# Attention and a routed feed-forward layer on one core: square roots, exponentials and turns moved in the last two stages

## The reference, cut to what matters

```python
# x: (4, 512, 256) fp32; attention: 16 query heads, 4 key/value heads, D = 128
q, k, v = x @ Wq, x @ Wk, x @ Wv              # k and v repeated for 4 query heads each
y     = softmax(rope(q) @ rope(k).T * D**-0.5, causal) @ v
o_gla = scan over t of  S = S * exp(g_t) + ks_t v_t ;  o_t = qs_t S
        # qs, ks = softmax of q, k over D;  g = log_sigmoid(k) / 16
x = layernorm(x + (0.5 * y + 0.5 * o_gla) @ Wo)
# feed-forward: 8 experts, each 256 -> 176 -> 256, a token takes its top 2
w = softmax(x @ gate_w.T);  top_w, top_i = top_k(w, 2)
f = sum over the 2 experts of  top_w * ((silu(x @ Wg) * (x @ Wu)) @ Wd)
x = layernorm(x + f)                          # (v - mean) / sqrt(var + 1e-5)
```

## Time and profile before

| | us |
|---|---|
| median of 3 runs | 973.99 (973.38 to 974.23) |
| the profiled execution | 972.46 |
| its span in the trace | 970.6 |
| PE busy | 925.6 (95%) |
| ACT busy | 661.7 (68%) |
| DVE busy | 653.2 (67%) |
| POOL busy | 634.5 (65%) |
| mean granted PE clock | 0.985 of full |

### The profile page before, as it was taken

How to read it: one execution, slowest core, us unless ns; L and a number is a source line. 1 busy time by engine, 2 the same in 40 slices (tenths; PEclk the granted TensorE clock), 3 DMA queues, 4 the chain that set the end, 5 groups by cost and what they waited for, 6 DMA issues and landing times.

```text
span 970.6 us, 18411 instructions
## 1 busy us (share of the span) xinstructions
PE 925.6 (95%) x5347; PEld 717.4 (74%) x5347; DVE 653.2 (67%) x1598; ACT 661.7 (68%) x2138; POOL 634.5 (65%) x609
## 2 busy tenths in 40 slices
PE   7899999999999999999999999999999988998991
PEld 4677778787878787878878777777778766776770
DVE  4776767676767676767676969676978774452284
ACT  6677777777777777777777767786768674454452
POOL 6868685767565657676767768775658883536452
PEclk9899999999999999999999999999999999999996
DMA  7101100000000000900000000010102111233363
GB/s 252 34 17 34 39 1 1 7 12 6 1 0 0 0 0 6 252 18 1 1 2 1 1 6 8 1 63 1 63 2 74 50 59 55 82 89 118 111 197 114
DMA packets 34066, 43.20 MB, mean 45 GB/s; under 512 B 3772, under 2 KB 27966, under 8 KB 33856
## 3 DMA queue, kind: packets, MB, share of 16 engines
q1 hardware_dynamic: 30240, 33.76, 12.0%
q0 software_dynamic: 3744, 8.43, 2.5%
HBM read 25.58 MB, written 18.43 MB: 45 GB/s over the span
## 4 chain that ended last, share of the span: by engine, by line
PE 86%; ACT 4%; DVE 4%; issue 3%; DMA 2%; POOL 1%; another core or an unknown queue 0%; POOLq 0%; SPq 0%; DVEq 0%; ACTq 0%
PE OA L597 13%; PE PR L480 12%; PE S L550 11%; PE MS L570 10%; PE S L579 7%; PE S L696 5%; PE OA L559 5%; PE OA L713 4%; PE OA L590 4%; PE PR L526 3%; PE PR L520 3%; PE S L541 1%; PE MS L509 1%; DMA acc<-in_x_rows 1%; ACT eqk L828 1%
## 5 line engine op out<-in xcount | busy, mean ns | idle before, releaser
L1500 POOL TENSOR_TENSOR qd<-eqk,eg 128x512 f32<-128x512 f32 x63 | 74.9, 1189 | 161.8 <-issue 155.4
L597 PE MATMUL OA<-wT,V 128*128 128x512 f32 x320 | 149.2, 597 | 0.0
L790 ACT ACTIVATE S<-S,nm 128x128 f32<-128x128 f32 (+3 forms) x256 | 126.9, 496 | 28.7 <-DVE nm L1003 25.4
L828 ACT ACTIVATE eqk<-qkv,nmx 128x128 f32<-128x128 f32 x320 | 124.4, 396 | 3.4 <-DVE nmx L1078 2.9
L1003 DVE TENSOR_REDUCE nm<-S 128x2 f32<-128x256 f32 (+3 forms) x128 | 102.0, 817 | 30.7 <-PE S L550 24.7
L1488 POOL TENSOR_TENSOR eqk<-eqk,rse 128x640 f32<-128x640 f32 x63 | 79.6, 1264 | 52.8 <-DVE rse L1121 31.5
L597 PEld LDWEIGHTS OA<-wT,V 128*128 128x128 f32 x320 | 59.7, 191 | 69.4 <-issue 68.9
L1037 DVE TENSOR_TENSOR pr<-S,rl 128x256 f32<-128x256 f32 (+3 forms) x128 | 105.5, 824 | 5.0
L1477 POOL TENSOR_TENSOR rp<-qkv,cos 128x640 f32<-128x640 f32 x64 | 99.6, 1556 | 6.6 <-ACT qkv L818 4.9
L1480 POOL TENSOR_TENSOR rp<-rp,rt 128x640 f32<-128x640 f32 x64 | 99.6, 1556 | 5.0
L1477 POOL TENSOR_TENSOR rt<-qkv,sin 128x640 f32<-128x640 f32 x64 | 99.3, 1552 | 0.0
(11 more groups left out here) (174 smaller groups left out, 2499.4 us busy)
## 6 DMA issues: line engine op xcount, KB each, us to landing
qkv<-slot_x SPq DMA_DIRECT2D x46, 129.0 KB
pr<-plane SPq DMA_DIRECT2D x16, 256.0 KB, 2.8
gu_w<-in_wgu SPq DMA_DIRECT2D x8, 352.0 KB, 3.4
slot_x<-zero SPq DMA_DIRECT2D x2, 1290.0 KB, 9.4
stage<-in_wqkv SPq DMA_DIRECT2D x6, 384.0 KB, 3.5
xraw<-in_x_cols SPq DMA_DIRECT2D x16, 128.0 KB, 2.4
acc<-in_x_rows SPq DMA_DIRECT2D x1, 2048.0 KB, 11.5
dn_w<-in_wdn SPq DMA_DIRECT2D x8, 256.0 KB, 4.2
```

The lines of the kernel that those rows point to most:

```text
L597: last = pe.matmul(OA[:, :], V[:, j, :], wT[:, j, :], start=(c == 0 and j == 0), stop=(j == c))
L790: nc.scalar.activation(S[:, h, 0:n], S[:, h, 0:n], ACT.Exp, bias=nm[:, h:h + 1], scale=1.0, accum_out=ls[:, h:h + 1]).then_inc(s_exp, 1)
L828: last = nc.scalar.activation(eqk[:, par, h * 128:(h + 1) * 128], qkv[:, c % C, h * 128:(h + 1) * 128], ACT.Exp, bias=nmx[:, h:h + 1], sca ...
```

## The change

There are five edits.

1. In the last step of attention PE turns the weights first and then the two first slot tiles; ACT copies in the same order.
2. ACT loads the table of silu behind the last exponentials of attention, ahead of `weights_out`, in place of at the first silu. The router's exponentials of the last batch go from q = 11 to q = 47, the loop's last round, and with them the table loads around them: one for the exponential, then one for the square root.
3. The weights of the last batch (`route_weigh(1)`) go from q = 17 to behind the last `shift2` of the third batch, ahead of the combination of tile 12.
4. For the last batch ACT takes the square root (`deviations`) and DVE the reciprocal; POOL's last two `rs2` are gone.
5. In the last group DVE clamps the gates ahead of both halves of `normalise` in all steps that clamp, where before it did so only at c = 1 (of all groups).

```diff
@@ PE, step
-                if not n1:
-                    turn_x(0)
-                    turn_x(1)
                 turn_weights(g, c)
+                if not n1:
+                    turn_x(0)
+                    turn_x(1)
@@ ACT, step
                 if not n1:
-                    x_out(0)
-                    x_out(1)
+                    act.preload_act_table_set("silu_and_others")
                 ...
                 weights_out(g, c)
+                if not n1:
+                    x_out(0)
+                    x_out(1)
@@ ACT
+            def deviations(i):
+                v, r = (x[:, 2 * i:2 * i + 2] for x in (ve[2], rstd[2]))
+                act.wait_ge(s_ve[2], i + 1)
+                nc.scalar.activation(r, v, ACT.Sqrt).then_inc(s_rs[2], 1)
@@ ACT, the loop over q and behind it
-                if q == 11:
+                if q == NT + 1:
+                    act.preload_act_table_set("natural_log_exp_and_others")
                     router_exp(3)
+                    act.preload_act_table_set("sqrt_and_others")
                 if q >= 40:
                     norm2(q - 40)
             for t in range(NT + 2 - 40, TILES - 1):
+                if t in (3 * TPB, 3 * TPB + 2):
+                    deviations(t // 2)
                 norm2(t)
@@ DVE, step
-                if n1 and c == 1:
+                clamp_first = c == 1 or last
+                if n1 and clamp_first:
                     clamp_gates(g, c + 1)
                 normalise(g, c, 0)
-                if n1 and c != 1:
+                if n1 and not clamp_first:
                     clamp_gates(g, c + 1)
@@ DVE, shift2
                 dve.wait_ge(s_rs[2], 2 * n + h + 1)
+                if n == 3:
+                    nc.vector.reciprocal(rstd[2][:, i], rstd[2][:, i]).then_inc(s_rc, 1)
+                    dve.wait_ge(s_rc, h + 1)
@@ DVE, the loop over q and behind it
-                if q == 17:
-                    route_weigh(1)
                 ...
             shift2(2, 1)
+            route_weigh(1)
             for t in range(3 * TPB, TILES):
@@ POOL, at the end
             rs2(2, 1)
-            rs2(3, 0)
-            rs2(3, 1)
```

More of the change, by code:

```diff
@@ L263, in layer_kernel @@
         s_mark, s_back, s_bf = sem("s_mark"), sem("s_back"), sem("s_bf")
-        s_last = sem("s_last")
+        s_last, s_rc = sem("s_last"), sem("s_rc")
         s_yg = [sem(f"s_yg{i}") for i in range(4)]
@@ L661, in step @@
                     output(g - 1 if c == 0 else g, C - 1 if c == 0 else c - 1)
+                turn_weights(g, c)
                 if not n1:
@@ L664, in step @@
                     turn_x(1)
-                turn_weights(g, c)
                 if k in TURN_AT:
```

## The result

The changed kernel takes 970.9 us (median of 13 runs, 966.53 to 972.01) against 973.71 for the kernel before (13 runs beside it, 971.44 to 975.39). The ratio is 0.9969 with a 95% interval of 0.9957 to 0.9981: 0.31% faster, 2.8 us by the medians. The forecast was 973.3 and its range began at 971.4. A second comparison, at the end of the experiments, gave 968.16 against 971.69, a ratio of 0.9962 (0.9949 to 0.9976). All times from here on come with the median of the kernel before that was measured beside them. The ratio of a comparison is not exactly that of the two medians, so the two can differ by some tenths of a microsecond.

A forecast was written before the change was run, and what follows sets the result against it. The prediction took PE as the bound through the loop, then DMA, DVE, ACT and stores. Its terms, +0.43 - 1.0 - 0.1 = -0.67, shifted the median from 973.99 to 973.3 us, range 971.4 to 975.0.

The forecast's parts named there:

- Edit 1, +0.43: Last step of attention: four slot-tile transposes leave a wait and add their whole length, +0.43 us (bounds 0 to 0.86).
- Edit 2, -1.0: Loop around q = 11: without the router's two table loads, 1.0 us less (bounds 0.73 and 1.60); early silu load gains 0.
- Edit 3, 0: Ahead of tile 12's combination: the last batch's weights fit into DVE's wait for rows, 1.1 us left; cost 0.
- Edit 5, 0: Last group, c = 2: PE's clamp wait shrinks, but it then waits for POOL's features; 0 (bounds 0 to -0.5).
- Edit 4, -0.1: Last tiles: square root on ACT, reciprocal on DVE shorten the path to the last norm2; -0.1 us (bounds -0.3 to +0.2).
- Behind the loop PE has nothing to do; a DMA, then DVE, then one ACT instruction and the stores set the end: Kernel's end, after the loop: those units were taken to set the finish; no size given.
- terms inside their bounds: Whole kernel: the forecast case of 973.3 us, from 972.4 to 974.0, with chance 0.61.
- the clock rival: Last step of attention: PE's half clock returns later after a longer idle stretch, +1.4 us, total 974.7; chance 0.10.
- The loads cost their whole length: Loop at q = 11: removing the loads gains all 2.79 us ACT spends, time 971.5; chance 0.05.
- The tail is not covered: Loop's end: new table loads slower by 1.1 us or more delay DVE's tile 12, time 974.3; chance 0.03.
- Stalls of an unknown queue: Loop, near 879.87: a stall of about 1.7 us goes (971.6, chance 0.14) or one comes (975.0, chance 0.07).

The follow-up runs named there:

- x9: Kernel before with only the last group's clamps moved ahead of both normalise halves; 968.24 us against 969.33, one run each.
- x10: Kernel before with POOL's eight sends of the last batch five rounds later (from q = 20, not 15); 976.05 us against 969.33, one run each.
- x1: Kernel before with only the last batch's square roots on ACT and reciprocals on DVE, POOL's last two powers gone; 969.69 us against 973.29.
- x11: The changed kernel itself, measured a second time; 968.16 us against 971.69 for the kernel before, ratio 0.9962.
- x7: Changed kernel with the two slot tiles turned ahead of the weights again, silu's table load behind their copies; 967.38 us against 972.64 for the kernel before.
- x12: Kernel before with a one-column memset nobody reads as POOL's last instruction, issued when DVE finishes the very last tile; 973.2 us against 971.69.
- x3: Changed kernel plus an unread POOL memset, issued when the variance of tiles 14 and 15 is there; 972.24 us against 973.29 for the kernel before.
- x8: Like x7, but SP stores the very last tile ahead of tile 14; 967.01 us against 972.64 for the kernel before.
- x2: Changed kernel with POOL taking the powers of tiles 12 to 15 again; 972.94 us against 973.29 for the kernel before.
- x4: Changed kernel plus an unread POOL memset, issued when the variance of tiles 12 and 13 is there; 968.85 us against 973.29 for the kernel before.
- x6: Kernel before with only the two slot tiles turned behind the last weights; 972.94 us against 972.64.

## Why the prediction was wrong

Its steps, one by one:

- **Edit 1, +0.43: right.** 0.43 by the distances above, with the clock's part taken out.
- **Edit 2, -1.0: right.** -0.99 between silus, and -1.0 for edits 2 and 3 alone. The round of 3.11 shows that `prefix` keeps its 0.6, as the prediction had it.
- **Edit 3, 0: right.** 1.29 us of DVE's wait were left behind it, 1.1 were forecast. It was not timed without edit 2.
- **Edit 5, 0: right.** POOL's features release the turn, and the last step's weights keep their distance (x9). The times of x9, one execution of each kernel, could not tell.
- **Edit 4, -0.1: wrong by a factor of 30.** Its direct path came out as forecast: from the combination of tile 12 to the last `norm2` it is 7.62 us in the traces with POOL's power (7.77 in the one of before and 7.88 in x10) and 7.48 or 7.49 with the square root, so -0.14. But the step "Behind the loop PE has nothing to do; a DMA, then DVE, then one ACT instruction and the stores set the end" was false. POOL's DRAIN set it, 3.23 us behind the stores. The term should have been -3.23 - 0.14 = -3.4; x1 measured -3.6. So the step that failed is the path behind the last `norm2`: the prediction put the time from there to the end at nothing to gain, and 3.23 us of it were POOL's.

In the second trace of the change (x11, with about the same low clock and the same stalls as the one of before) the forecast for the stores came true: they were in at 967.19 before and at 966.51 there, 0.68 earlier; the prediction had 0.67. The span went from 970.65 to 966.72, by 3.93, and the terms give -3.23 - 0.99 + 0.43 - 0.14 = -3.93. That they agree to the hundredth is luck: this execution came to the last step's weights 0.15 later than that of before, its stalls were 0.10 shorter, it lost 0.11 from the last `down` to the combination of tile 12, and its combination was shorter by 0.29 and not by 0.14, since the trace of before lies 0.15 above the others there.

In the first trace of the change only 2.6 of this are left. These are the differences that make its last `norm2` begin 0.60 later than in the trace of before:

- -0.41: PE came to the last step's weights earlier, which has nothing to do with the change, as shown at x9;
- +0.43 for edit 1, and +0.30 for a half-clock stretch of 3.41 instead of 2.82;
- -0.99 for edit 2;
- +0.62 for longer stalls between q = 18 and 30;
- +0.94 for PE's last `down`, which fell into half clock (below);
- -0.29 in the combination.

Together they are +0.60, and with the 3.23 that POOL no longer adds the span is 2.6 shorter. The two comparisons, -2.8 and -3.5 by their medians, have intervals of -4.2 to -1.9 and -5.0 to -2.3, so both hold the 3.9. Why the medians lie somewhat under it isn't settled. The last `down` fell into half clock in five of the fourteen traces, those of after, x7, x9, x10 and x12, of which the last three have the loop's end of before, and this costs 0.7 to 0.9 in such executions.

**The sign was in the trace of before.** Stores issued at 964.80 and 965.19 that need 1.7 us at least are in at about 967, and the prediction itself had a span of 970.6. Had I subtracted the one from the other, 3.6 us with no owner would have asked for an explanation. I had carried the view of the chain to its last row and taken that row for the end.

**Two slips in its working.** The forecast's part of the chances is given as "terms inside their bounds (972.4 to 974.0)", but the bounds as stated add up to -2.4 and +0.33, that is 971.6 to 974.3; even so the measured 970.9 lies below them. And PE's clock did not fall in the idle stretch ahead of 815.35, as the clock rival says, but while PE was at the four transposes of the slot tiles, with 3.36 of the low 3.41 us busy (columns: window, length, PE busy and count, clock, DMA share, GB/s):

```profile
814.76:818.17 3.41, 3.36 (x15) 0.50 0.09 31
```

**The rivals.** The range ended at 971.4, and the cases below it were stalls or loads, so the way it went had been given a chance of 0.23, for the wrong reasons. *The clock stays low longer* did happen: 6.10 us at half clock behind the first transpose in x3, 6.05 in x8, 6.02 in x12, each costing about 1.6. But x8 and x12 have the order of before there, and five traces with the new order (after, x2, x4, x6, x11) had 2.75 to 3.41, so it isn't the change that brings it. The Trainium skill, page "TensorE: Matmul & The Clock Gate", section "What's actually happening", says that the window in which the chip watches PE runs free of the kernel. The traces agree as far as they go: with the same instructions, the low stretch began 0.86 behind the first transpose of the weights in one execution of the change (after) and 0.66 ahead of it in the other (x11). *The loads cost their whole length*: no, 0.99. *The tail is not covered*: no, it was by 1.29. *Stalls of an unknown queue* moved and changed their size, but as much without the change as with it. Summed over q = 18 to 30, what the silus lose against 2.487 us per round is 4.45 before, 5.07 after, 4.0 to 5.8 in the others, and nothing in x9 (and in x10 only the wait that it made itself). In the comparison of these two the kernel before took 969.33, 2.4 to 4.4 us less than its medians in the others. Fewer stalls may be why times differ from one comparison to another; no run shows it, and what the stalls wait for stays open.

## What to carry to other kernels

Ahead of any sum for the end of a kernel, close its account: last store issued, plus its landing, against the end of the span; a remainder of microseconds with every engine idle has an owner that the views don't list. In a kernel like this one POOL's last instruction should come well ahead of the last store (here it would be enough if it ended some 3.4 us before the start of the last `norm2`, 6.47 - 3.04), even at the price of an instruction or two more on other engines. An engine that is off the path all the way can still set the end through what it does behind its last instruction.

## What the runs showed of the hardware

In all fourteen traces POOL's DRAIN ends 6.45 to 6.47 us behind the end of its last instruction, after a power of 0.69 us as after a memset of 0.10 us, and with POOL's last DMA instruction ending 0.7 us ahead of that end (after) as well as 12 us ahead (x12). The last DRAINs of DVE, ACT and PE end 0.03 to 0.05 us behind the last instruction of their engine. POOL has another DRAIN at the start of the kernel, behind four memsets of 0.10 us, and that one ends 0.05 us behind the last of them. So a DRAIN of POOL is not long as such. What makes the last one long stays open: in between POOL issued 78 DMAs, the same number in every version, and no run leaves them out.

The Trainium skill, page "VectorE: DVE Perf Modes", section "The DRAIN you can't avoid", speaks of DRAINs that the runtime puts around a kernel and gives some 12 ns for them, on all five engines. Those of this case belong to the kernel's own program (their records carry a line of it), so they may be of another kind. SP's last one took 7 ns, and POOL's record is 6.6 to 8.4 us long; that figure can't be used for POOL's.

PE's clock can fall near the loop's end, before PE has finished. In the trace of after it was at 1.00 until 948.9 and at 0.50 from there on. PE stood idle at that moment, as it had for 1.09 us in the round before, and the last `down` (L713) took nearly twice as long as the one ahead of it:

```profile
946.82 1.13 PE L713 MATMUL OA<-dn_w,am 128*128 x4 [1.09 <-ACT am L921]
...
949.25 2.07 PE L713 MATMUL OA<-dn_w,am 128*128 x4 [1.09 <-ACT am L921]
```

In the trace of before, with the same waits, the clock was still full there:

```profile
949.29 1.13 PE L713 MATMUL OA<-dn_w,am 128*128 x4 [1.09 <-ACT am L919]
```

The half-clock stretch in the last step of attention is 3.41 us long in the traces of before and after, and 6.83 in x3 (first the trace of after, then x3; columns as in the window above):

```profile
815.80:819.21 3.41, 3.41 (x16) 0.50 0.00 0
```

```profile
814.53:821.36 6.83, 6.10 (x23) 0.50 0.06 18
```

In x3 PE was busy for 6.10 of the 6.83 us and still had half its clock throughout.
